# A fused two-layer attention and feed-forward kernel: one attended tile computed ahead of the second batch's projection, with scratch, spills, squares and folds placed anew

## The reference

```python
x = x + fake_quant(layernorm(x)) @ fake_quant(ctx)            # first layer, attention
x = x + streams_ffn(layernorm(x))                             # first layer, 4 streams, Sinkhorn
Q, K = x3 @ Wq.T + bq, ctx @ Wk.T + bk                        # x3 = layernorm(x)
x = x + softmax(Q @ K.T / 32) @ ctx                           # second layer, attention
y = layernorm(x)
x = x + lora(silu(lora(y, gate)) * lora(y, up), down)         # second layer, feed-forward
```

## Time and profile before

| | |
|---|---|
| time of three runs | 1170.32, 1171.17 (median), 1172.99 us |
| the profiled execution | 1175.09 us, its span 1173.3 us |
| TensorE busy | 1103.4 us, 94% of the span |
| VectorE, ScalarE busy | 798.7 us (68%), 484.4 us (41%) |
| mean granted clock of TensorE | 0.984 of full speed |

### The profile page before, as it was taken

One profiled execution on the slowest core, in us unless ns is written; L12 is line 12 of the kernel. 1 busy time (PEld: TensorE's weight loads), 2 busy tenths in 40 slices (PEclk: granted clock), 3 DMA queues, 4 the chain that ended last, 5 costly groups with the idle time before them and its releaser, 6 DMA issues.

```text
span 1173.3 us, 16032 instructions
## 1 busy us (share of the span) xinstructions
PE 1103.4 (94%) x6150; PEld 541.9 (46%) x6150; DVE 798.7 (68%) x1600; ACT 484.4 (41%) x731; POOL 154.2 (13%) x184
## 2 busy tenths in 40 slices
PE   4786999899999999958999999999999999999998
PEld 2353544654445444424444444444444444444443
DVE  8999988889994187877767676767676664333330
ACT  6896753773145135654343434344343341111110
POOL 4884340073004010000000000000001000000000
PEclk9997999999999999988999999999999999999999
DMA  9720000123032028685202111121211275322200
GB/s 370 265 96 1 2 1 1 73 66 114 1 108 86 1 66 240 115 189 110 72 36 72 41 68 62 46 72 37 72 37 39 89 188 123 116 65 65 64 16 27
DMA packets 80061, 97.19 MB, mean 83 GB/s; under 512 B 57776, under 2 KB 58416, under 8 KB 79984
## 3 DMA queue, kind: packets, MB, share of 16 engines
q1 hardware_dynamic: 79984, 96.16, 27.1%
HBM read 76.22 MB, written 6.29 MB: 70 GB/s over the span
## 4 chain that ended last, share of the span: by engine, by line
PE 70%; DVE 18%; ACT 5%; DMA 3%; issue 2%; SPq 2%; ACTq 0%; DVEq 0%
PE PAIR L2517 32%; PE PAIR L2169 10%; PE PAIR L2170 10%; PE PAIR L2171 10%; DVE X L1557 2%; PE PAIR L2472 1%; DVE BST L1355 1%; DVE PAIR L1509 1%; DVE POOL L1383 1%; PE PAIR L2549 1%; DVE BST L1356 1%; SPq L492 1%; DVE X L1426 1%; DVE LORA L1508 1%; DVE LORA L1510 1%
## 5 line engine op out<-in xcount | busy, mean ns | idle before, releaser
L2169 PE MATMUL PAIR<-POOL 128*128 128x512 f16 x672 | 255.5, 380 | 2.2 <-DVE POOL L1600 2.2
L2170 PE MATMUL PAIR<-POOL 128*128 128x512 f16 x672 | 255.5, 380 | 0.0
L2171 PE MATMUL PAIR<-POOL 128*128 128x512 f16 x672 | 255.4, 380 | 0.0
L2517 PE MATMUL PAIR<-XT,POOL 128*128 128x512 f16 x1008 | 230.1, 382 | 16.2 <-DMA XT<-POOL 16.2
L2517 PEld LDWEIGHTS PAIR<-XT,POOL 128*128 128x128 f16 x1008 | 98.3, 98 | 132.7 <-issue 19.4
L2517 PE MATMUL PAIR<-X,POOL 128*128 128x512 f16 x504 | 115.7, 379 | 0.0
L2171 PEld LDWEIGHTS PAIR<-POOL 128*128 128x128 f16 x672 | 65.7, 98 | 80.1 <-issue 1.1
L2169 PEld LDWEIGHTS PAIR<-POOL 128*128 128x128 f16 x672 | 65.6, 98 | 69.4 <-DVE POOL L1600 4.3
L2170 PEld LDWEIGHTS PAIR<-POOL 128*128 128x128 f16 x672 | 65.7, 98 | 65.3 <-issue 0.4
L1065 ACT ACTIVATE POOL<-STG 128x1024 f16<-128x1024 f32 (+2 forms) x32 | 25.3, 790 | 169.7 <-DVE STG L1758 169.7
L1758 DVE SCALAR_TENSOR_TENSOR STG<-STG,PAIR 128x1024 f32<-128x1024 f32 (+2 forms) x32 | 28.3, 885 | 89.8 <-PE PAIR L2549 86.6
(11 more groups left out here) (305 smaller groups left out, 1711.6 us busy)
## 6 DMA issues: line engine op xcount, KB each, us to landing
STG<-in_gate_w SPq DMA_DIRECT2D x21, 512.0 KB, 3.6
STG<-in_up_w SPq DMA_DIRECT2D x21, 512.0 KB, 4.3
STG<-in_ctx_t SPq DMA_DIRECT2D x16, 512.0 KB, 4.1
STG<-in_ctx SPq DMA_DIRECT2D x16, 512.0 KB, 4.2
STG<-in_down_w SPq DMA_DIRECT2D x16, 512.0 KB, 3.5
POOL<-in_ctx SPq DMA_DIRECT2D x12, 512.0 KB, 11.1
X<-in_x SPq DMA_DIRECT2D x8, 512.0 KB, 9.6
out_t<-T4B SPq DMA_DIRECT2D x16, 256.0 KB, 2.0
```

The lines of the kernel that those rows point to most:

```text
L2169: e.matmul(dst, l_hi, r_hi, start=first, stop=False)
L2170: e.matmul(dst, l_hi, r_lo, start=False, stop=False)
L2171: return e.matmul(dst, l_lo, r_hi, start=False, stop=last)
L2517: i = e.matmul(dst, blk[:, a_, k, :], src[:, b_, k, :], start=(opens and k == 0 and n == 0), stop=(k == KD // 2 - 1 and n == 2), skip_grou ...
```

## The change

TensorE computes `attend(3)`, the first batch's last attended tile, before `project(1, ...)` instead of between `fold(0)` and `fold(1)`; `EARLY` becomes 4, which gives it its bank pair there, and VectorE's `add_attended(3)` and its statistics move with it, so that one `norm_rest(0, 4)` does for four tiles. The pieces' scratch is placed anew: only t = 0 and t = 3 now share the early region at 80 KB, while t = 1 and t = 2 lie in AT's region. The spill of X goes ahead of `turn_fourth` in SyncE's queue. ScalarE's square of tile 4 is taken between the splits of the first batch. `fold(4)` and `fold(5)` stand ahead of S1 instead of ahead of S3 and A22. VectorE's `gate_first(0)`, `difference(2, T3)` and two block splits change places. The pieces of the diff stand in this order: the tables, SyncE, ScalarE (`piece_hi`, then its order), VectorE's order, TensorE's order.

```diff
-EARLY = 3
+EARLY = 4
-    return {T1: 3 * t + 3, T2: 2 * t + 7, T3: 4 * t + 2, T4: t + 13}[p]
+    return {T1: 2 * t + 5, T2: 3 * t + 4, T3: 2 * t + 8, T4: t + 13}[p]
-            return region((80, 80, 64, 72)[t] + 4 * group, 4)
+            return region((80, 64, 72, 80)[t] + 4 * group, 4)
...
-                if n == SLOTS:
-                    for g in range(BT):
-                        e.wait_ge(x3_ok, g + 1)
-                        e.dma_start(x_keep[g * P:(g + 1) * P, :], X[:, g, :]).then_inc(spilled, 16)
...
                     turn_weights(BT + 3)
+                    for g in range(BT):
+                        e.wait_ge(x3_ok, g + 1)
+                        e.dma_start(x_keep[g * P:(g + 1) * P, :], X[:, g, :]).then_inc(spilled, 16)
                     for u in range(BT):
                         turn_fourth(u)
...
                 if t == 1 and p == T1:
+                    e.wait_ge(av_p, NT)
+                elif t == 3 and p == T1:
                     wait_turned(e, 0)
-                elif t == 2 and p == T1:
-                    e.wait_ge(av_p, NT)
...
-            norm_root(0, 3)
+            norm_root(0, 4)
...
-            norm_root(3, 4)
...
             fourth_normal(0)
+            fourth_hi(0)
             fourth_normal(1)
+            fourth_hi(1)
+            spread(4)
             fourth_normal(2)
+            fourth_hi(2)
             fourth_normal(3)
-            for u in range(BT):
-                fourth_hi(u)
-            spread(4)
+            fourth_hi(3)
...
             add_attended(2)
+            stats_of(2)
+            add_attended(3)
...
-            stats_of(2)
+            stats_of(3)
...
-            norm_ask(0, 3)
-            norm_rest(0, 3)
+            norm_ask(0, 4)
+            norm_rest(0, 4)
             weights_lo(6)
             slab_add(0)
...
-            add_attended(3)
-            stats_of(3)
             weights_lo(7)
-            attended_terms(3)
...
             spread_rest(4)
+            block_lo(0, "S3")
+            block_lo(0, "A22")
             fourth_lo(2)
             fourth_lo(3)
-            block_lo(0, "S3")
-            block_lo(0, "A22")
...
             spread_rest(6)
-            gate_first(0)
             piece_lo(1, T1)
...
             add_attended(7)
             difference(e, 2, T1)
-            difference(e, 2, T3)
+            gate_first(0)
             spread_rest(7)
...
             piece_lo(3, B22)
+            difference(e, 2, T3)
             difference(e, 3, T2)
...
             attend(2, 4, KP)
+            attend(3)
             for n in range(KD // 2):
                 project(1, n)
...
             score(7)
             fold(0)
-            attend(3)
             fold(1)
             attend(4, 0, 3)
             fold(2)
...
             product(1, "A12")
+            fold(4)
+            fold(5)
```

More of the change, by code:

```diff
@@ L1954, in _ @@
                     maximum(0)
-            def attended_terms(g):
-                norm_ask(g, g + 1)
-                norm_rest(g, g + 1)
             mix_factors(1)
@@ L2720, in _ @@
             product(1, "A12")
+            fold(4)
+            fold(5)
             for j in range(TAIL):
                 for n, (at, name) in enumerate(products(j)):
-                    if at == j and name in (("S3", "A22") if j == 0 else ("S2", "S4")):
+                    if j and at == j and name in ("S2", "S4"):
                         ahead = 2 * j + 4 + (name in ("S4", "A22"))
```

## The result

| | before | changed |
|---|---|---|
| median of 4 runs each | 1171.32 us (1170.32 to 1172.99) | 1179.68 us (1176.36 to 1182.13) |
| ratio, 95% interval | | 1.0061 [1.0035, 1.0086] |
| the profiled execution, its span | | 1182.13 us, 1180.3 us |
| TensorE's mean granted clock | | 0.984 |

The change makes the kernel 0.6% slower.

The account below looks back on a forecast made before the run. TensorE was taken as bound by its 16.2 us wait at S1 for a DMA into XT. fold(2)'s wait 8.23 + clock 2.2 - earlier pieces 4.4 gave +6.0 us on 1171.17: 1177.2 us, range 1172.8 to 1180.2.

Parts of the forecast that it names:

- The chain of the earlier trace: Work up to slab_add(0), said to start at the last score; shifted 10.36 us to 474.61, so fold(2) waits 8.23 us.
- The rival: At fold(2): slab_add(0) set by a DMA or earlier VectorE work, so no wait; -4.4 us, 1166.8 us; 7 in 100.
- The upper bound: Behind fold(2)'s wait: at most 2.5 us lost to the half clock; 2.2 us was taken.
- The last attended tile: End of attention on TensorE: done at 515.3 us against 504.84, 10.4 us late from fold(2)'s wait and the clock.
- the 18.95 us: Time from the first piece of t = 1 to S1, kept as in the profile before.
- cost and gain nothing: VectorE behind slab_add(0): losing add_attended(3), its statistics and one norm there was put at no effect.
- the new scratch gives nothing: Pieces of t = 1: another link holds them, S1 stays 26.67 us behind the last tile; +10.5 us, 1181.7 us; 10 in 100.
- the baseline of 26.67 us: Distance from the last attended tile to S1 in the kernel before.
- 4.4 us: Gain at the first piece of t = 1: 3.3 us behind the last attended tile instead of 7.72.
- The folds moved: fold(4) and fold(5) ahead of S1: up to 0.9 us possible, taken as 0 because A22 would wait for it.
- A12's covered wait: A12 of hidden tile 1 waits 3.9 us for gate_first(0), costing nothing because S1 isn't due before 537.
- the likeliest case's own range: Whole kernel: 1175.7 to 1178.7 us, from 1.6 to 2.5 us of clock and 0.8 us either way for DMA landing.

Follow-up runs that it names:

- e0: The changed kernel timed again with no edit; 1178.37 us, ratio 1.0050.
- e2: The changed kernel with attend(3) and its VectorE work back between the folds, all else as changed; 1169.89 us, ratio 0.9973.
- e10: The changed kernel with ScalarE's square of tile 4 and VectorE's two block splits back at their old places; 1178.04 us, ratio 1.0055.
- e8: The changed kernel with VectorE's gate_first(0) ahead of the pieces of t = 1 again; 1180.27 us, ratio 1.0078.
- e1: The kernel before with only attend(3) and its VectorE work moved ahead of project(1); 1181.17 us, ratio 1.0070.
- e4: The changed kernel with 36 matmuls, their result overwritten, filling TensorE's wait ahead of fold(2); 1176.32 us, ratio 1.0037.
- e9: The changed kernel with fold(4) and fold(5) ahead of S3 and A22 of hidden tile 0 again; 1178.34 us, ratio 1.0063.
- e11: The changed kernel with 20 matmuls, their result overwritten by S1, filling the wait ahead of S1; 1178.36 us, ratio 1.0058.
- e7: e2 with ScalarE's keep_first(0) behind the first four pieces of t = 1 instead of ahead of them; 1165.77 us, ratio 0.9946.
- e6: The kernel before with only the spill of X moved ahead of the four transposes (turn_fourth); 1169.03 us, ratio 0.9982.

## Why the prediction was right, and where it was not

**fold(2).** Predicted: a wait of 8.23 us, with no second one at fold(3). Measured: 8.21 us here and in e0, 7.95 to 8.67 in the others with the move. e2, without the move, has no wait at the fold. The chain of the earlier trace rows, moved by 10.36 us, was the right way to price it. Its start was named wrongly: it comes from score(5) and a context tile's landing, not from the last score. The price held because score(5) moves with project(1) too, and because the landing took nearly the same time in both traces (4.84 and 4.92 us). The rival said that a DMA might set this chain; one does stand in it, but its issue hangs on score(5), so it fell. The landing is what makes the wait differ between kernels that are equal up to here: 4.56 us and a wait of 7.95 in e10, 4.92 and 8.21 in the changed kernel, 5.23 and 8.50 in e8, 5.40 and 8.67 in e1.

**The clock.** Predicted 2.2 us between bounds of 0 and 2.5. Measured 1.94 us, and e4 shows that it is the clock. It was to fall after about 4 us; it fell after 5.4 us in this trace, and the wait of 8.21 was long enough for either. The upper bound was too low: in e8, e9 and e11 the distance from fold(2) to fold(3) is 7.15 to 7.26 us, so 2.8 to 2.9 us are lost. I had taken the bound from the one return of the clock that the trace before shows.

**The last attended tile.** Predicted 515.3; measured 516.34, or 515.15 without the 1.19 us from ahead of the stage.

**S1.** Predicted 3.3 us from there to the first piece and 18.95 from the piece to S1; measured 3.29 and 538.53 - 519.63 = 18.90. S1 was to start at 537.5 and starts at 537.34 in the same count. The sum was right, but its attribution was wrong in three steps. The first: "on VectorE one difference of 0.6 us goes behind the last group 0 piece and gate_first(0), as long, comes in", with no effect on the 18.95 us. With gate_first(0) left in place S1 would have come 2.0 us later (e8), because it waits for A12 and VectorE's halves wait behind it; the trace of before had shown no such cost because the pieces were later there anyway. I had kept the 18.95 us, which holds only thanks to that move. The second: the other 2.4 us needn't come from scratch and spill here, since with the move e1 has them without either. The third is why: for add_attended(3), its statistics and its norm, which VectorE no longer does behind slab_add(0), I had written "cost and gain nothing", but they bring the work on the first batch's rows 2.6 us forward (e1). So "the new scratch gives nothing", the rival, was half true as a mechanism, but not at its price, since the baseline of 26.67 us no longer held. That 4.4 us came out right is in part luck: the change held every edit that they needed, and I had put them all down to one.

**S2 and A22.** Predicted 0 to 0.6 us lost at S2. Measured: S2 comes 5.51 us behind S1 where it was 5.03, so 0.48 us; from fold(0) to A22 it is +6.20 in all. The folds moved were worth nothing, as predicted (e9), and S1's slow matmuls cost nothing (e11). A12's covered wait was predicted at 3.9 us and is 3.74.

**The time.** Predicted +6.0, in the stage +6.20 and +6.09. The median, 1179.68 us, is inside the range of 1172.8 to 1180.2, by 0.5 us, and 1.0 above the likeliest case's own range; the second measurement, 1178.37, is inside that too as it was written. The terms named for that range (-0.6 and +0.3 us for the clock, 0.8 either way for the landing) add up to 1175.8 to 1178.3 only, not to 1178.7. Executions of the changed kernel differ by up to 5.8 us (1176.36 to 1182.13), and what the start of the program contributes to that (two groups 4 us apart) was not in my range.

## What to carry to other kernels

Work that looks free to move may be the cover of a wait that no list shows: before moving it, measure the slack of the next semaphore behind its old place (2.13 us here against 10.36 us moved), and add what the clock takes after a wait of that length. Work that goes from one engine's queue with it can pull other chains forward (2.6 us here), which the sum must hold too. Where several edits attack the same chain, each must be priced with the others in place: here three edits gave the same 2.4 us once, and a fourth was needed for the next 2.0. An instruction that waits for an engine should stand behind the work that others wait for, as gate_first(0) on VectorE and keep_first(0) on ScalarE show.

## What the runs showed of the hardware

The same kernel, or kernels that are equal up to this point, lose between 1.6 us (e0) and 2.9 us (e11) at half clock after a wait of 8.0 to 8.7 us. The time at which the clock falls differs too. In the changed kernel it fell 5.4 us into the wait, and in e1, whose wait began at 463.21, after 2.5 us:

```profile
465.50:466.00 0.50, 0.00 (x0) 0.73 0.93 106
```

In e9 the clock stays at 0.50 from the restart for at least 5 us:

```profile
470.50:476.00 5.50, 5.08 (x18) 0.50 0.71 133
477.00:477.50 0.50, 0.50 (x4) 1.00 0.00 0
```

The Trainium skill (TensorE: Matmul & The Clock Gate, Part 1: The HAM clock gate) says of a kernel's start that the number of slow matmuls differs from run to run of the same kernel. The traces here show the same behind a wait in mid-program: 6 matmuls of 128x512 ran slowly behind fold(2) in e0, 7 in the first trace of the same kernel, and 12 in e11.

A wait of only 3.74 us cost the clock as well. These are windows of the changed kernel around A12 of hidden tile 1, whose wait began at 524.27; up to 527.5 the clock was 1.00:

```profile
527.50:528.00 0.50, 0.00 (x0) 0.72 1.16 217
528.00:531.00 3.00, 2.99 (x8) 0.50 0.67 127
```

It was free of cost only because S1 had to wait anyway. In e7 the same wait is 1.14 us, and A12 runs at full clock (12 matmuls in 2.75 us).

The Trainium skill (DMA: Bandwidth & Descriptors, Queues, rings and completion order) has descriptors consumed in ring order. A spill of four tiles ahead of four transposes did not delay these by more than 0.2 us (e6). As its last part was issued over 6 us earlier and such a part lands in 4.2 us in the median there, its data was probably through, so the run doesn't speak against the rule.
